# Four network layers on one core: a head's turns placed between two weight products, square-root tables loaded at the ends of stages, idle products behind the recurrent steps

## The reference

```
x = L0(x)   # layer norm, 2-D Fourier transform, block-diagonal complex product per frequency, inverse, + x; then layer norm, MLP 96 -> 384 -> 96 with GELU, + residual
x = L1(x)   # root-mean-square norm, SiLU branches u and v, long convolutions over rows and over columns whose coefficients come from two small networks, gate, product, + x
x = L2(x)   # layer norm, input product, two bidirectional GRUs over the 256 places, gate silu(z), product, + x
x = L3(x)   # the same as L2 with other weights
```

```
r = sigmoid(gx_r + h @ Wr);  z = sigmoid(gx_z + h @ Wz)
n = tanh(gx_n + r * (h @ Wn));  h = (1 - z) * n + z * h
```

## Time and profile before

| | |
|---|---|
| median of three runs | 955.68 us (954.44 to 956.04) |
| profiled execution | 954.95 us, span 952.8 us |
| instructions | 55077 |
| PE, DVE, ACT, POOL busy | 95%, 85%, 74%, 3% of the span |
| the steps of L2 and L3 | about 173 to 542 us and 570 to 939 us |

### The profile page before, as it was taken

One profiled execution on the slowest core, in us unless ns is written; L12 is line 12 of the kernel. 1 busy time (PEld: TensorE's weight loads), 2 busy tenths in 40 slices (PEclk: granted clock), 3 DMA queues, 4 the chain that ended last, 5 costly groups with the idle time before them and its releaser, 6 DMA issues. The chain is left out here.

```text
span 952.8 us, 55077 instructions
## 1 busy us (share of the span) xinstructions
PE 908.9 (95%) x22394; PEld 819.1 (86%) x22394; DVE 813.7 (85%) x5086; ACT 708.1 (74%) x4756; POOL 27.1 (3%) x18
## 2 busy tenths in 40 slices
PE   6799999999999999999999789999999999999996
PEld 6557886799999999999999759999999999999995
DVE  7575179788888889999999878888888899999996
ACT  4462954877777778888888657777777788888884
POOL 2001150000000000000000000000000000000000
PEclk9999999655555555555555585555555555555555
DMA  6000800000000000000000000000000000000001
GB/s 176 3 15 15 168 5 10 3 4 5 4 4 5 4 4 4 5 4 5 4 4 5 4 7 4 4 5 4 4 5 4 4 4 5 4 4 4 4 5 35
DMA packets 15007, 13.61 MB, mean 14 GB/s; under 512 B 12374, under 2 KB 13911, under 8 KB 14463
## 3 DMA queue, kind: packets, MB, share of 16 engines
q1 hardware_dynamic: 14753, 10.09, 4.5%
HBM read 9.25 MB, written 0.83 MB: 11 GB/s over the span
## 5 line engine op out<-in xcount | busy, mean ns | idle before, releaser
L1449 PE MATMUL L2s_cand_sum<-states,L_w_hidden 97*128 97x8 bf16 x2048 | 172.3, 174 | 0.0
L1449 PE MATMUL L3s_cand_sum<-states,L_w_hidden 97*128 97x8 bf16 x2048 | 172.1, 174 | 0.0
L1449 PE MATMUL L2s_reset_sum<-states,L_w_hidden 97*128 97x8 bf16 x2048 | 142.5, 180 | 2.6 <-DVE states L1293 1.7
L1449 PE MATMUL L3s_reset_sum<-states,L_w_hidden 97*128 97x8 bf16 x2048 | 142.4, 180 | 2.5 <-DVE states L1293 1.7
L1449 PEld LDWEIGHTS L2s_cand_sum<-states,L_w_hidden 97*128 97x128 f16 x2048 | 131.3, 105 | 0.0
L1449 PEld LDWEIGHTS L3s_cand_sum<-states,L_w_hidden 97*128 97x128 f16 x2048 | 131.1, 105 | 0.0
L1449 PE MATMUL L2s_keep_sum<-states,L_w_hidden 97*128 97x8 bf16 x2048 | 130.0, 174 | 0.0
L1449 PE MATMUL L3s_keep_sum<-states,L_w_hidden 97*128 97x8 bf16 x2048 | 130.0, 174 | 0.0
L1390 ACT ACTIVATE L2s_reset<-L2s_reset_sum 96x16 f32<-96x16 f32 x512 | 93.3, 182 | 46.4 <-PE L2s_reset_sum L1449 46.4
L1390 ACT ACTIVATE L3s_reset<-L3s_reset_sum 96x16 f32<-96x16 f32 x512 | 93.2, 182 | 46.4 <-PE L3s_reset_sum L1449 46.2
L1449 PEld LDWEIGHTS L3s_reset_sum<-states,L_w_hidden 97*128 97x128 f16 x2048 | 103.2, 110 | 27.8 <-DVE states L1293 4.9
(11 more groups left out here) (263 smaller groups left out, 3072.1 us busy)
## 6 DMA issues: line engine op xcount, KB each, us to landing
L_wih_raw<-in_L_wih SPq DMA_DIRECT2D x2, 1152.0 KB, 11.2
l_w_for_re<-in_L_w SPq DMA_DIRECT2D x1, 1728.0 KB, 10.5
L_w_hidden_raw<-in_L_whh SPq DMA_DIRECT2D x2, 576.0 KB
stream<-in_x SPq DMA_DIRECT2D x2, 384.0 KB, 4.0
out<-stream SPq DMA_DIRECT2D x4, 192.0 KB, 2.4
l_idft<-in_idft SPq DMA_DIRECT2D x1, 400.0 KB
rpe_lw<-in_rpe_lw SPq DMA_DIRECT2D x1, 384.0 KB
lagged<-coefs SPq DMA_DIRECT2D x16, 24.0 KB, 2.1
```

Source lines behind the costliest of these rows:

```text
L1449: return e.matmul(dst, weights.hidden[0:rows, wp, GATES * (2 * g + j) + gate, :], rhs, start=False, stop=False, skip_group_check=True)
```

## The change

It has five parts.

1. `warm` moves from each norm into `Stats`; it is set once at the start of the kernel (`prepare`), and `norm_scalar` runs only the root of `power`. A new `next_root`, a square root of `warm`, is ScalarE's last instruction in `mix_frequencies`, `mlp`, `toeplitz` and L2's `gru_output`, and its first in the kernel.
2. GpSimd's memset of one row of `forward` moves from L2's head to the end of GpSimd's program in `toeplitz`; `forward` is allocated before `toeplitz`.
3. In L2's head TensorE turns tiles 0 to 3 between weight products 0 and 1, and ScalarE runs `high(0)`, `input_high(0)`, `high(1)`, `input_high(1)` in place of `high(0)`, `high(1)`, `input_high(0)`, `input_high(1)`.
4. At the end of `gru_steps` TensorE waits until ScalarE has read group 0's sums of the last step and runs 8 idle products into `reset_bank[0]`, in both layers.
5. At the end of L2's `gru_output` TensorE waits for the first added bank and runs 6 idle products into it.

```diff
@@ norm_vector, Stats, norm_scalar
-    e.memset(n.warm[:], 1.0).then_inc(n.power_ready, 1)
+        self.warm = ctx.enter_context(nc.sbuf_tensor("warm", [P, 1], F32))
+def next_root(e, stats):
+    e.activation(stats.warm[:], stats.warm[:], ACT.Sqrt)
     e.wait_ge(n.power_ready, 1)
-    e.activation(n.warm[:], n.warm[:], ACT.Sqrt)
-    e.wait_ge(n.power_ready, 2)
     e.activation(n.root[:], n.power[:], ACT.Sqrt).then_inc(n.root_ready, 1)
@@ mix_frequencies, ScalarE: its first instruction
+                e.wait_ge(rpe.power_ready, 1)
+                next_root(e, stats)
                 norm_scalar(e, norm)
@@ prepare
+        e.memset(stats.warm[:], 1.0)
@@ toeplitz, GpSimd, at its end
+                e.memset(forward[C:C + 1, 0], 1.0)
@@ gru_input
-            if bias_rows is not None:
-                @block.gpsimd
-                def _(e):
-                    e.memset(forward[C:C + 1, 0], 1.0)
@@ gru_input, ScalarE
+                weights.high(e, *((0, banks[4]) if done == 0 else (2, banks[6])))
+                input_high(0)
                 if done == 0:
-                    for b in range(2):
-                        weights.high(e, b, banks[4 + b])
-                else:
-                    weights.high(e, 2, banks[6])
-                input_high(0)
+                    weights.high(e, 1, banks[5])
                 input_high(1)
@@ gru_input, TensorE
-                if done == 0:
-                    for b in range(2):
-                        weights.product(e, b, banks[4 + b])
-                else:
-                    weights.product(e, 2, banks[6])
+                weights.product(e, *((0, banks[4]) if done == 0 else (2, banks[6])))
...
-                turn(range(0, 8))
+                turn(range(0, 4))
+                if done == 0:
+                    weights.product(e, 1, banks[5])
+                turn(range(4, 8))
@@ gru_steps, TensorE, at its end
+                e.wait_ge(advanced[0], 5 * (SEQ - 1) + 3)
+                idle_products(e, reset_bank[0][:].rearrange("p a c s -> p (a c s)"), ident, 8)
@@ gru_output, TensorE, at its end
+                if out_dram is None:
+                    e.wait_ge(added, 1)
+                    idle_products(e, banks[0], ident, 6)
```

More of the change, by code:

```diff
@@ L95, in __init__ @@
         self.root = sb("root", [P, TILES])
-        self.warm = sb("warm", [P, 1])
         self.guess = sb("guess", [P, TILES])
@@ L313, in _ @@
             def _(e):
-                rpe.prepare(e)
+                rpe.prepare(e, stats)
                 for h in range(X_PARTS):
@@ L666, in link, with prepare @@
         e.wait_ge(self.chained, self.links)
-    def prepare(self, e):
+    def prepare(self, e, stats):
         self.link(e, e.memset(self.ones[:], 1.0))
+        e.memset(stats.warm[:], 1.0)
         e.memset(self.exponent[:], -0.5).then_inc(self.power_ready, 1)
@@ L720, in lagged_layout, with toeplitz @@
     return bass.AP(flat_coefs.tensor, octet * 2 * LAGS + axis * LAGS, [[1, SIDE], [8 * 2 * LAGS, OCTETS], [1, SIDE]])
-def toeplitz(nc, d, stream, ident, minus, coefs, lagged, lagged_loaded, weights, stats):
+def toeplitz(nc, d, stream, ident, minus, coefs, lagged, lagged_loaded, weights, forward, stats):
     with ExitStack() as ctx:
@@ L1042, in gru_layer @@
         gru_input(nc, d, layer, stream, ident, minus, weights, done, forward, states, gate, w_out, w_out_parts, w_loaded, stats, bias_rows)
-        gru_steps(nc, layer, weights, forward, states, gate, y, s_tok, s_parts)
-        gru_output(nc, layer, stream, s_parts, w_out_parts, stats, out_dram, stored)
+        gru_steps(nc, layer, ident, weights, forward, states, gate, y, s_tok, s_parts)
+        gru_output(nc, layer, stream, ident, s_parts, w_out_parts, stats, out_dram, stored)
 def gru_input(nc, d, layer, stream, ident, minus, weights, done, forward, states, gate, w_out, w_out_parts, w_loaded, stats, bias_rows):
@@ L1190, in _, with gru_steps @@
                     gate_low(i)
-def gru_steps(nc, layer, weights, forward, states, gate, y, s_tok, s_parts):
+def gru_steps(nc, layer, ident, weights, forward, states, gate, y, s_tok, s_parts):
     with ExitStack() as ctx:
@@ L1484, in _, with gru_output @@
                         add(KEEP, 0, 1, 1).then_inc(keep_summed[g], 1)
-def gru_output(nc, layer, stream, s_parts, w_out_parts, stats, out_dram, stored):
+                e.wait_ge(advanced[0], 5 * (SEQ - 1) + 3)
+                idle_products(e, reset_bank[0][:].rearrange("p a c s -> p (a c s)"), ident, 8)
+def gru_output(nc, layer, stream, ident, s_parts, w_out_parts, stats, out_dram, stored):
     with ExitStack() as ctx:
@@ L1524, in _ @@
                     last.then_inc(projected, 1)
-            if out_dram is not None:
+                if out_dram is None:
+                    e.wait_ge(added, 1)
+                    idle_products(e, banks[0], ident, 6)
+            if out_dram is None:
+                @block.scalar
+                def _(e):
+                    next_root(e, stats)
+            else:
                 @block.sync
@@ L1559, in build @@
         minus = ctx.enter_context(nc.sbuf_tensor("minus", [C, C], F16))
-        toeplitz(nc, d, stream, ident, minus, coefs, lagged, lagged_loaded, weights, stats)
         forward = ctx.enter_context(nc.sbuf_tensor("forward", [C + 1, 2, BATCH, SEQ], F16))
+        toeplitz(nc, d, stream, ident, minus, coefs, lagged, lagged_loaded, weights, forward, stats)
         states = [ctx.enter_context(nc.sbuf_tensor(f"states{g}", [C + 1, SEQ + 1, PER, 2], F32)) for g in range(GROUPS)]
```

## The result

The changed kernel took **949.36 us** (median of 4 runs, 948.32 to 951.19) beside 955.86 us before (954.44 to 956.81): ratio 0.9939, 95% interval 0.9922 to 0.9956. A second measurement (6 runs, 947.77 to 952.0) gave 0.9937 [0.9915, 0.9959]. So it is faster by about 6 us; forecast were 951.3 us and a range of 949.3 to 954.2. The profiled execution took 948.32 us with a span of 946.3; it is 6.5 shorter than the span of before.

What follows compares the result with a forecast made beforehand. The recurrent steps fill some 738 of 952.8 us and stay unchanged; only seams between blocks gain. Terms 0.9 + 0.15 + 0.7 + 1.9 + 0.4 = 4.05 us gave 950.9 profiled, 951.3 predicted, range 949.3 to 954.2.

Steps and rivals of the forecast that it cites:

- Sign and time: Whole kernel: faster 0.80, same 0.15, slower 0.05; 951.3 us, range 949.3 to 954.2.
- Seams before mlp, toeplitz: Block starts: 0 before mlp; before toeplitz the root runs earlier without its load, 0.9 us gained, bounds 0.7 and 0.95.
- The end of toeplitz: ScalarE's load and warm activation end 0.14 us before VectorE ends the block; uncovered, at most 1.5 us lost.
- The head of L2: Start of L2: root 1.6 us earlier, product 2 only 0.15 us earlier; gain 0.15, bounds -0.1 and 0.6.
- with no gap: it is the bound: L2's head: TensorE runs products, turns and product 2 without a gap, so it bounds the head.
- my bound of -0.1: L2's head, lower bound of the gain: rest 1 waits for high(1), one place later in ScalarE's order.
- The memset's new place: Toeplitz: GpSimd's memset beside VectorE's copies out of PSUM costs nothing or 1.58 us; taken as 0.
- Idle products behind the steps: After both layers' steps: 8 products take 3.49 us, delay 0.1; outputs gain 0.7 in L2, 1.9 in L3.
- the rise comes 3.3 to 6.8 us after a busy stretch begins: Both outputs: the full clock comes 3.3 to 6.8 us after TensorE's busy stretch begins, depending on the run.
- No early rise: Rival, chance 0.16: the clock counts anew from the output's start, both outputs gain nothing; 954.0 us.
- The head of L3: Start of L3: the root comes 1.1 us earlier, but product 2 may run at half clock; gain taken 0.4.
- But product 2 comes first: L3's head: product 2 precedes the first turn, taking 1.7 us at full clock or 3.4 at half.

Runs made afterwards that it cites:

- the short fp16 filling: Changed kernel with 43 fp16 products of 96 columns in place of the 8 fp32 idle products behind each layer's steps: 954.05 us, ratio 0.998.
- before again: The kernel before, unchanged, run for a second profile: 955.43 us (10 runs), ratio 0.9991.

## Why the prediction was right, point by point

- **Sign and time.** Right, the time 1.9 us below the forecast and 0.06 inside the range. Three terms were too small: the two outputs, which hang on the clock, and L3's head, which hangs on the root. With another mix of rises the time could as well have lain outside, so its place in the range is partly luck.
- **Seams before mlp, toeplitz.** 0 and 0.9 forecast, 0.93 measured; 0.85 came back when the loads were put back. The root now waits for power, as said.
- **The end of toeplitz.** Cover forecast 0.14, measured 0.11. The drain that the Trainium skill (ScalarE: Activation LUTs, What ACT_TABLE_LOAD costs) states did not show here either: the activation ahead ends at 153.31, the load runs 153.34 to 154.62, the next activation starts at 154.63. The page would have put this end 1.2 us late; the block ended on time.
- **The head of L2.** The sum, 0.15, was right (0.16), but by luck; the reason was wrong. The failed step is "with no gap: it is the bound". In the earlier trace rows eight turns take from 159.17 to the rests, 1.72 us in all; unhindered they take 0.87. The wait for rows was inside a grouped row, where no idle time is printed. So the early root alone was worth 0.81 us (15.96 to 15.15), and the new order took 0.65 of it back. I had forecast the gain as the order's. Inside the sum for the new order two errors cancelled as well: turns 4 to 7 took 0.11 each and not 0.15, and the rests 0.66 in all and not 0.45, by the wait of rest 1 (0.22) that my bound of -0.1 had named.
- **The memset's new place.** 0, as taken; what was left open is settled: the copy beside it, out of PSUM, lasted 0.69. The Trainium skill (SBUF — State Buffer, Who interferes with whom) has a VectorE instruction with at most one SBUF input and outside the two-port modes undisturbed by GpSimd; the copy, which reads no SBUF, agrees. Power, with one SBUF input, was stretched to 1.79 beside the same memset again; by the page's sentence it would have to run in a two-port mode, which no run here shows.
- **Idle products behind the steps.** Their length (3.49 forecast, 3.76 and 3.30 measured) and the delay (0.1, 0.13) were right. The step with "the rise comes 3.3 to 6.8 us after a busy stretch begins" was not: 6 of 16 rises came at 2.66 to 3.22, 4 at over 9. L2's output brought 1.07 for 0.7 although the rise came 5.06 us after the first idle product, the very middle that I had taken (546.2 less 541.14): mis-sized was VectorE's part, with the first add 1.67 us after the output's start for 1.8, and 6.62 from there to the last statistics for 6.8. L3's brought 2.91 for 1.9, in an execution with a rise at 2.66: the products took 2.49 us less for 2.0, and the last store landed 0.4 us sooner behind them, where I had taken 0.1 off. That 0.4 is no effect shown: from the end of the last add to the end of the span it took 2.51 to 3.11 us over all 14 profiles, in before as in the changed kernels.
- **"No early rise".** I gave this rival 0.16 for both outputs together. For both outputs of one execution it came in none of the eight profiles with these idle products. Output by output it exists: 4 of 16, costing 0.6 to 1.3 us in L2 and 1.6 to 2.4 in L3 against the outputs with an earlier rise. With the up to 3 us by which mix differs, it accounts for a spread like that of 947.8 to 952.0: of the two profiled runs of one kernel, 948.32 and 949.85, the second has a mix longer by 1.8 us and the quicker output. That the unprofiled runs differ for the same two reasons is argued, not shown.
- **The head of L3.** The term was mis-sized, 0.4 for 1.11. The step "But product 2 comes first", from which "The gain is 1.1 or -0.5" follows, was wrong. The root came 0.21 us after the block's start for 1.33 before, 1.12 earlier, and the head got 1.11 shorter, with product 2 at 1.93 us and at 2.60 alike: the sixteenth turn began 5.62 us into the block in both profiles of the changed kernel (6.72 before). So up to there the root and the rows behind it set the pace, not product 2. "More often slow than fast" missed too: the head lasted 13.39 to 13.41 in 9 of the 10 profiles that have the six idle products and the early load. In five of the nine the clock stayed up; in four it fell 1.1 to 1.6 us after product 2 began, for 3.4 us, and the head was no longer. Only longer stays at half, of 6.83 us, came with a longer head. The exception (15.14) had the short fp16 filling; the clock fell 1.5 us after product 2's start and stayed down for 6.83.
- **Steps change their length.** No: the earlier trace rows and its answer agree, and the 0.35 and 0.44 us between the block lengths lie within what the same steps show from profile to profile (372.6 to 373.6). Before has two profiles only, 373.24 to 373.37 us, within that range.

## What to carry to other kernels

A row that groups instructions can hide waits: compare its time per instruction with the fastest of its kind before calling an engine gapless. Where two changes act on one chain, put each back alone: here the new order was a loss of 0.65 us under the cover of a gain of 0.81, and the version with the old order has the shortest head, though a whole-kernel time with a spread of 2 us can't show it. A gain that rests on the clock is a chance per execution and wants several profiles. And an engine that starts a block without a wait need not be the block's bound: in L3's head a product 0.7 us longer cost nothing.

## What the runs showed of the hardware that I had not expected

- How long TensorE was recorded busy ahead of a rise does not tell when it comes: 3.6 us of fp16 products brought no early rise in 4 outputs of 4 (7.95 to 9.64 us after the first), 3.3 to 3.8 us of fp32 products did in 12 of 16, 2.05 us of fp32 products in none of 2 (9.24 and 9.38). The cause is open.
- With the eight fp32 products the time to the rise lies in three ranges, 2.7 to 3.2, 4.2 to 5.7 and 9.2 to 9.4 us, for the same instructions, and never between them in 16 outputs.
- A small VectorE instruction (0.17 us) beside GpSimd's memset lasted as long as the memset, 1.76 to 1.79 us, and a copy of 0.69 us out of PSUM beside the same memset was not stretched.
- The Trainium skill (TensorE: Matmul & The Clock Gate, What's actually happening) calls the first rise variable from run to run for the same kernel; these runs agree, and an output at half the clock from first product to last (6.97 us of the 7.84, before again) goes further than that.
